# A threshold search inside an attention: the counts, the totals and the update take other places in the queues

## What is computed

```python
def _topk_mask(ck, k):
    probs = jax.nn.softmax(ck, axis=-1)
    _, idx = jax.lax.top_k(probs, k)
    b = jnp.arange(probs.shape[0])[:, None]
    return jnp.zeros_like(probs).at[b, idx].set(1.0)
...
new_mask = _topk_mask(ck, ITER_SIZE)
combined = jnp.clip(history + new_mask, 0.0, 1.0)
novelty = (combined - history).sum(axis=1).mean() / ITER_SIZE
done_next = jnp.logical_or(done, novelty < R)
```

## Time and profile before

| | |
|---|---|
| median of three runs | 1364.15 us (1363.6 to 1365.42) |
| the profiled execution's own time | 1362.49 us |
| its span | 1360.4 us |
| mean granted TensorE clock | 0.967 of full speed |
| TensorE busy | 1226.8 us, 90% |
| VectorE, ScalarE, GpSimd busy | 941.5, 795.5, 577.5 us |

### The profile page before, as it was taken

How to read it: one execution, slowest core, us unless ns; L and a number is a source line. 1 busy time by engine, 2 the same in 40 slices (tenths; PEclk the granted TensorE clock), 3 DMA queues, 4 the chain that set the end, 5 groups by cost and what they waited for, 6 DMA issues and landing times. The chain is left out here.

```text
span 1360.4 us, 37961 instructions
## 1 busy us (share of the span) xinstructions
PE 1226.8 (90%) x13719; PEld 877.9 (65%) x13719; DVE 941.5 (69%) x2042; ACT 795.5 (58%) x2101; POOL 577.5 (42%) x613
## 2 busy tenths in 40 slices
PE   1799999999999986969888888499999979999996
PEld 0466666666666653437766677378888857777775
DVE  6466766767767754758989889489999966334341
ACT  1588788787787761226776676356666633333332
POOL 3587665665665645022222222343333324333443
PEclk9899999999999997969999999789999989999998
DMA  8000000000000000000000000200000000000000
GB/s 213 11 2 1 0 0 0 0 0 0 0 0 0 0 1 1 0 8 10 9 8 8 8 7 7 64 2 1 0 0 0 1 2 9 9 8 8 8 8 17
DMA packets 22740, 14.71 MB, mean 11 GB/s; under 512 B 6378, under 2 KB 21610, under 8 KB 22540
## 3 DMA queue, kind: packets, MB, share of 16 engines
q1 hardware_dynamic: 22520, 13.75, 3.8%
q10 hardware_dynamic: 148, 0.01, 0.0%
HBM read 11.66 MB, written 2.10 MB: 10 GB/s over the span
## 5 line engine op out<-in xcount | busy, mean ns | idle before, releaser
L694 POOL TENSOR_TENSOR r_norm<-ssm,mhalf 128x24 f32<-128x24 f32 x32 | 134.8, 4213 | 161.8 <-DVE ssm L599 161.8
L1929 ACT ACTIVATE moe_hid<-psum 128x512 f32<-128x512 f32 x128 | 76.3, 597 | 136.7 <-PE psum L1863 136.6
L537 ACT ACTIVATE l_probs<-psum,l_n_max 128x248 f32<-128x248 f32 x256 | 117.0, 480 | 57.5 <-DVE l_n_max L617 57.5
L2087 POOL TENSOR_TENSOR moe_acc<-moe_acc,moe_prod 128x512 f32<-128x512 f32 x64 | 81.4, 1272 | 146.4 <-DVE moe_prod L2043 146.4
L1873 PEld LDWEIGHTS psum<-w,moe_hid 128*128 128x128 f32 x1024 | 123.1, 192 | 26.8 <-issue 26.5
L2043 DVE TENSOR_TENSOR moe_prod<-psum,moe_combine 128x512 f32<-128x512 f32 x64 | 44.2, 691 | 134.9 <-PE psum L1873 134.8
L1873 PE MATMUL psum<-w,moe_hid 128*128 128x128 f32 x1024 | 123.4, 275 | 0.0
L1863 PE MATMUL psum<-moe_moe_hT,w 128*128 128x512 f32 x256 | 121.6, 602 | 0.0
L1734 POOL TENSOR_TENSOR l_QX<-l_qT,own_slots 128x512 f32<-128x512 f32 x32 | 33.3, 1040 | 184.0 <-ACT l_qT L1557 184.0
L1734 POOL TENSOR_TENSOR mla_QX<-mla_qT,own_slots 128x512 f32<-128x512 f32 x32 | 33.3, 1040 | 135.5 <-ACT mla_qT L1557 135.5
L701 POOL TENSOR_TENSOR qkn<-qk,r_norm 128x1536 f32<-128x1536 f32 x32 | 88.3, 2761 | 2.5
(11 more groups left out here) (309 smaller groups left out, 3422.3 us busy)
## 6 DMA issues: line engine op xcount, KB each, us to landing
X<-x_in SPq DMA_DIRECT2D x8, 256.0 KB, 4.8
out_dram<-moe_acc SPq DMA_DIRECT2D x32, 64.0 KB, 1.5
CT<-ctx_in SPq DMA_DIRECT2D x8, 240.0 KB, 5.9
l_cT<-ctxT_in SPq DMA_DIRECT2D x32, 60.0 KB, 1.8
w<-w_in SPq DMA_DIRECT2D x1, 1024.0 KB, 5.3
wm<-wm_in SPq DMA_DIRECT2D x1, 768.0 KB, 4.4
wp<-wp_in SPq DMA_DIRECT2D x1, 768.0 KB, 6.5
wkv<-wkv_in SPq DMA_DIRECT2D x1, 512.0 KB, 5.1
```

Source lines behind the costliest of these rows:

```text
L537: e = act.activation(probs[u][:, h, :], psum[:, 2 * u + h // 2, (h % 2) * K:(h % 2 + 1) * K], ACT.Exp, bias=n_max[u][:, h:h + 1], accum_ou ...
L694: pool.tensor_tensor(r_norm[:, :], ssm[:, :], mhalf[:, 0:3 * H], ALU.pow).then_inc(s["norm_inverted"], 1)
L1929: act.activation(hid[i % RING][:, :], psum[:, 2 + i % BANKS, :], ACT.Silu).then_inc(activated[i], 1)
L2087: pool.tensor_tensor(a[:, :, :], a[:, :, :], prod[e % 2][:, :, :], ALU.add).then_inc(summed[e], 1)
```

## The change

The counts get new places on ScalarE: trials 0 and 1 directly behind `exp_b` of the odd step, trial 2 in front of `exp_b` of the even step. On TensorE the total moves from behind `turn_input` to behind the last `multiply_v` of the same even step, in front of `scores`. On VectorE the digit is read between `invert_sums` and `scale_out`; `invert_sums` of an even step now waits for the total as well. The three instructions of `next_trials` leave VectorE; four instructions on GpSimd take their place, each waiting for the one before, at the end of GpSimd's body of the even step. `second_half` stays on VectorE and moves behind `max_a`.

```diff
@@ TensorE @@
-                def total_trials(k, n):
+                def total_trials(k):
                     if round_there(k):
                         wait(pe, tried, k + 1)
-                        wait(pe, out_scaled, n + 1)
                         pe.matmul(psum[:, 6, 3 * P:3 * P + 12], ...
...
                     turn_input(n + 1)
-                    if router and par == 0:
-                        total_trials(k - 1, n - 2)
                     project(n - 2)
...
                     multiply_v(n - 1, 1 - par, 3)
+                    if router and par == 0:
+                        total_trials(k - 1)
                     scores(n + 1, 1 - par)
@@ ScalarE @@
                         if d == 0:
                             wait(act, trials_ready, k)
+                            if isinstance(k, int) and k == ROUNDS:
+                                wait(act, halved, 4)
...
                     copy_k(n + 1, 1 - par)
+                    if router and par == 0:
+                        try_number(k - 1, 2)
                     exp_b(n, par)
                     if router and par == 1:
+                        try_number(k, 0)
                         try_number(k, 1)
                     copy_group(act.copy, act, n, 0)
-                    if router and par == 1:
-                        try_number(k, 2)
                     exp_a(n + 1, 1 - par)
-                    if router and par == 0:
-                        try_number(k, 0)
@@ VectorE @@
-                def read_digit(k, n):
+                def read_digit(k):
                     if round_there(k):
-                        wait(dve, projected, n + 1)
                         wait(dve, totalled, k + 1)
+                        wait(dve, below_made, k)
...
-                def next_trials(k):
-                    if round_there(k):
-                        t = search
-                        wait(dve, trials_ready, k)
-                        wait(dve, digit_read, k + 1)
-                        dve.tensor_scalar(t["bias"][:, :], t["offsets"][:, :], t["below4"][:, :], t["digit4"][:, :], ALU.add, ALU.subtract)
-                        dve.tensor_scalar(t["per_unit"][:, :], t["per_unit"][:, :], 4.0, None, ALU.mult)
-                        i = dve.tensor_scalar(t["below4"][:, :], t["below4"][:, :], t["digit4"][:, :], 4.0, ALU.subtract, ALU.mult)
...
                     copy_group(dve.tensor_copy, dve, n - 1, 3)
-                    if router and par == 0:
-                        read_digit(k - 1, n - 2)
                     add_projection(n - 2)
                     max_b(n, par)
                     take_stats(n - 2)
-                    if router and par == 0:
-                        next_trials(k - 1)
                     shift_b(n, par)
...
+                    if router and par == 0 and round_there(k - 1):
+                        wait(dve, totalled, k)
                     invert_sums(n - 1)
+                    if router and par == 0:
+                        read_digit(k - 1)
                     scale_out(n - 1)
                     max_a(n + 1, 1 - par)
+                    if router and par == 0 and isinstance(k, int) and k == ROUNDS:
+                        second_half()
@@ GpSimd @@
+                def next_trials(k):
+                    if round_there(k):
+                        t = search
+                        wait(pool, digit_read, k + 1)
+                        wait(pool, trials_ready, k)
+                        if isinstance(k, int) and k == ROUNDS:
+                            wait(pool, halved, 4)
+                        pool.tensor_tensor(t["below"][:, :], t["below4"][:, :], t["digit4"][:, :], ALU.subtract).then_inc(below_made, 1)
+                        wait(pool, below_made, k + 1)
+                        pool.tensor_tensor(t["bias"][:, :], t["offsets"][:, :], t["below"][:, :].broadcast_to([P, 3]), ALU.add).then_inc(bias_made, 1)
+                        wait(pool, bias_made, k + 1)
+                        pool.tensor_tensor(t["below4"][:, :], t["below"][:, :], t["four"][:, :], ALU.mult).then_inc(below4_made, 1)
+                        wait(pool, below4_made, k + 1)
+                        pool.tensor_tensor(t["per_unit"][:, :], t["per_unit"][:, :], t["four"][:, :], ALU.mult).then_inc(trials_ready, 1)
...
                     spread_q(n + 1, 1 - par)
+                    if router and par == 0:
+                        next_trials(k - 1)
                     later_scales(n)
```

More of the change, by code:

```diff
@@ L1253, in search_tiles @@
                 tried=sb("tried", [P, 3, Q4], BF16), count=sb("count", [P, 3]), totals=sb("totals", [P, 12]), digit4=sb("digit4", [P, 1]),
-                offsets=sb("offsets", [P, 3]), bias=sb("trial_bias", [P, 3]), below4=sb("below4", [P, 1]), per_unit=sb("per_unit", [P, 1]),
+                offsets=sb("offsets", [P, 3]), bias=sb("trial_bias", [P, 3]), below=sb("below", [P, 1]), below4=sb("below4", [P, 1]), four=sb("four", [P, 1]), per_unit=sb("per_unit", [P, 1]),
                 positive=sb("positive", [P, 1]), sign=sb("sign", [P, 1]), wanted=sb("wanted", [P, 1]), high=sb("high", [P, 1]),
@@ L1350, in _ @@
                     first_trials(dve, t)
+                    dve.memset(t["four"][:, :], 4.0)
                     dve.wait_ge(logits_done, 1)
@@ L1426, in attention16 @@
         halved = sem("halved")
+        below_made = sem("below_made")
+        bias_made = sem("bias_made")
+        below4_made = sem("below4_made")
         def row(T, n):
@@ L1652, in take_stats @@
                         dve.bn_stats(row(stats6, n), row(XO, n)).then_inc(x_stats, 1)
-                def read_digit(k, n):
+                def read_digit(k):
                     if round_there(k):
-                        wait(dve, projected, n + 1)
                         wait(dve, totalled, k + 1)
+                        wait(dve, below_made, k)
                         dve.tensor_scalar(search["totals"][:, :], psum[:, 6, 3 * P:3 * P + 12], search["wanted"][:, :], None, ALU.is_ge,
                                           ALU.add, accum_out=search["digit4"][:, :]).then_inc(digit_read, 1)
-                def next_trials(k):
-                    if round_there(k):
-                        t = search
-                        wait(dve, trials_ready, k)
-                        wait(dve, digit_read, k + 1)
-                        dve.tensor_scalar(t["bias"][:, :], t["offsets"][:, :], t["below4"][:, :], t["digit4"][:, :], ALU.add, ALU.subtract)
-                        dve.tensor_scalar(t["per_unit"][:, :], t["per_unit"][:, :], 4.0, None, ALU.mult)
-                        i = dve.tensor_scalar(t["below4"][:, :], t["below4"][:, :], t["digit4"][:, :], 4.0, ALU.subtract, ALU.mult)
[L1669 to L1673, removed]
                 def second_half():
                     t = search
+                    dve.wait_ge(trials_ready, ROUNDS)
+                    dve.tensor_scalar(t["high"][:, :], t["below4"][:, :], -0.0625, 0.5, ALU.mult, ALU.add).then_inc(halved, 1)
                     dve.wait_ge(halved, 1)
-                    dve.tensor_scalar(t["high"][:, :], t["below4"][:, :], -0.0625, 0.5, ALU.mult, ALU.add).then_inc(halved, 1)
-                    dve.wait_ge(halved, 2)
                     dve.scalar_tensor_tensor(t["low_here"][:, :], t["key"][:, :], t["high"][:, :], t["low"][:, :], ALU.is_equal,
@@ L1682, in second_half @@
                     dve.tensor_scalar(t["above"][:, :], t["key"][:, :], t["high"][:, :], 65536.0, ALU.is_gt, ALU.mult).then_inc(halved, 1)
-                    dve.wait_ge(halved, 4)
+                    dve.wait_ge(halved, 3)
                     dve.tensor_tensor(t["key"][:, :], t["low_here"][:, :], t["above"][:, :], ALU.add)
-                    first_trials(dve, t).then_inc(trials_ready, 1)
+                    first_trials(dve, t).then_inc(halved, 1)
                 def body(n, par, k):
```

## The result

The change takes the median from 1364.8 to 1344.7 us, a ratio of 0.985 (95% interval 0.983 to 0.987).

A forecast was written before the change was run, and what follows sets the result against it. Queues waiting on each other leave TensorE some 32 us idle in the search attention. Savings 5.5 + 1.4 + 2.1 + 2.2 = 11.2 us take 1362.5 to 1351.3; with the median 1.7 above, 1353 us, range 1345 to 1364.

The forecast's parts named there:

- first rival: No new stall: `turn_input` need not wait for GpSimd; double step 13.8 us, gain 31 us, 1333 us; 7%.
- Update on GpSimd: a new stall: Late update delays `centre`, `norm_input`: `turn_input` at t0 + 4.13 (t0: start of the total), not t0 + 2.61; stall 1.52 us.
- fourth rival: Shorter GpSimd waits: gaps 0.08 us instead of 0.16 in the loop, double step 14.9 us, 1348 us; 14%.
- TensorE needs 4.40 us: Time from `turn_input` to `scores` on TensorE, taken as 713.70 - 708.63 - 0.67, used twice in the 15.30 us double step.
- Loop: Eleven double steps in the loops, each 15.30 us instead of 15.80: 11 x 0.50 = 5.5 us less.
- Written out: The two written-out double steps (rounds 0 and 13), 14.87 us instead of 15.56 each: 1.4 us less.
- Second half: The one double step with `second_half`, 15.5 us instead of 17.58: 2.1 us less.
- The end: Rounds 14 and 15, no `turn_input` behind them: waits at the total and most of 0.67 us go, 2.2 us less.
- the forecast of the clock: TensorE's granted clock stays 1.00, stall costs only its length; rival, clock halves behind each stall: up to 62 us, 1415; 2%.
- Update dearer: Rival: GpSimd's four update instructions take 0.40 us each, giving 1364 us (11%), or 0.55, giving 1373 us (8%).
- Count late: Rival: counts late at the total's new place, TensorE waits 0.4 us there in 14 rounds: 5.6 us, 1359 us; 8%.

The follow-up runs named there:

- The late update: The changed kernel with the GpSimd update moved one body later, behind `norm_input` of the odd step, in front of `spread_q`: 1334.2 us, ratio 0.977 to the kernel before.
- the second wait in the experiment: The changed kernel with an already satisfied second wait ahead of the second, third and fourth update instruction: 1346.7 us, 2.0 us more than the change.
- the kernel with the counts alone: The kernel before with only count 0 moved, to stand with count 1 behind `exp_b` of the odd step; total and update as before: 1358.2 us, ratio 0.9955.
- longer update: The changed kernel with four more dependent 128x1 products on GpSimd in the update chain: 1370.7 us, ratio 1.0045 to the kernel before.
- the kernel with the update behind `max_a`: The changed kernel with the update back on VectorE as three instructions, behind `max_a` of the even step, GpSimd's four removed: 1336.6 us, ratio 0.980.

## Why the prediction was right or wrong

**Right: the mechanism.** The three waits go, and one takes their place, of `turn_input` for `norm_input` behind the update. The late update shows that it is the only one in the loop: without it the double step is 13.70 us, where I had 13.8 for my first rival. The stall then costs 14.52 - 13.70 = 0.82 us in a double step, where I had 1.52. The first rival's time, 1333, is what a kernel without the stall really takes (1334.2); it just isn't this change.

**Wrong: the step "Update on GpSimd: a new stall", mis-sized by 0.55 us.** I had `turn_input` at t0 + 4.13; it comes at 702.80 - 699.22 = 3.58. Term by term:

- Reciprocal at t0 + 0.43, not 0.53: 0.10. I took 0.14 us for VectorE to follow TensorE; here it starts 0.04 after the total's modelled end, close behind the copy of the values.
- Digit read by t0 + 1.44, not 1.65: another 0.11. The reading takes 0.14 us from start to end behind a running reciprocal, not the 0.24 of the earlier trace rows, where VectorE had idled in front of it.
- From the first update instruction to `centre` 0.96 us (700.82 to 701.78), not 1.28: 0.32. The instructions took 0.19 to 0.20, as said. The three gaps are 0.08, not the 0.16 of the earlier trace rows: 0.25 of the 0.32. That row has two waits in front of it, the last three of the update one each, and the second wait in the experiment brought most of the difference back. I had named 0.08 as my fourth rival, and gave it 14%. The other 0.07 are the instructions' 0.03 and a `centre` that starts 0.04 before the last of them ends.
- The rest is 0.02.

**Wrong: "TensorE needs 4.40 us", mis-sized by 0.24 in a double step.** I took a step with a wait in it and subtracted the wait. In the change it is shorter: 4.32 from `turn_input` to total (694.90 to 699.22) and 4.24 in the odd step (702.80 to 707.04). The subtraction was not the fault: in the kernel with the counts alone that wait is gone, and the odd step still takes 709.86 - 705.48 = 4.38. The cause of the 0.24 stays open.

**Together** they make 0.55 + 0.24 = 0.79; the double step came 15.30 - 14.52 = 0.78 us below the forecast.

**The sum, by its own terms**, from the input transposes. Loop: 11 x 1.28 = 14.1 us (forecast 5.5). Written out: 222.49 before, 826.07 - 622.22 = 203.85 after, so 18.64 in all; less 14.1 and the second half's 17.58 - (739.12 - 723.93) = 2.39, there remain 2.15 (1.4). Second half 2.4 (2.1). The end, with `project` of the last entry at 863.74 before and 843.80 after: 19.74 - 17.73 = 2.0 (2.2). That is 20.7 against 11.2, and nearly all of the miss is in the loop. Of the 20.7 the spans of the two profiled executions show 1360.4 - 1342.9 = 17.5: the changed kernel comes to this stretch 0.7 us later and takes 2.4 us more behind it, 1.35 of them in the first products of the mixture of experts (6.61 us against 5.26). No run tells why, and the medians' 20.1 is no check on the 20.7.

**The clock: right in the time, weak in the reason.** The granted clock of the changed kernel is 1.00 in the stretch, with its waits of 0.72 us. But I argued from one row, the 2.26 us of the earlier trace rows, that a wait of this kind leaves the clock alone. The longer update's 1.78 us did not, and in the kernel with the counts alone the very same wait, 2.25 us long, dropped it. One execution in which a thing did not happen was no bound, and that the forecast of the clock came true was in part luck. The Trainium skill (TensorE: Matmul & The Clock Gate, section "A second HAM failure mode: psum-queue depth-cycling") warned of a TensorE that stops for moments again and again. The trace of the longer update agrees in part: the clock fell behind 7 of its 14 waits.

**Rivals.** No new stall: wrong, the wait is in the list 14 times. Update dearer: wrong, 0.19 to 0.20 us each. Count late: wrong, no wait at the total. Shorter waits on GpSimd: right for the three gaps inside the update, 0.25 of the 0.55; the gap before the update and the one before `norm_input`, each with two waits, were 0.16. The lower end of my range, 1345, lay 3 us below this rival taken alone; here its gaps, the earlier digit and the shorter steps all went the same way.

## What to carry to other kernels

When work moves to an idle engine, look at what stands behind it in that engine's queue: in front of `centre`, with the digit late, the update cost 10.5 us, and one body later it made no wait in the loop. A chain of small steps is priced by its gaps as much as by its instructions; take the gap from a row with the same number of waits. Waits with different causes nearly add here, so it is worth removing them one by one, and looking each time at what the removal puts in front of something else.

## What was not expected of the hardware

The small VectorE instruction of the update took 0.90 us in the kernel before, but 0.28 at the same shape in the kernel with the update behind `max_a`. The timeline of GpSimd in the kernel before, its last update on VectorE with the listing of all 16 (shortest, median and longest in ns), and VectorE in the other kernel:

```profile
703.80 1.04 POOL L1734 TENSOR_TENSOR l_QX<-l_qT,own_slots 128x512 f32<-128x512 f32 x1 [5.40 <-ACT l_qT L1557]
```

```profile
860.49 0.27 DVE L1666 TENSOR_SCALAR trial_bias<-offsets,below,digit 128x3 f32<-128x3 f32 x1
...
L1666 DVE TENSOR_SCALAR trial_bias<-offsets,below,digit x16: 272/894/901, 625.0 to 860.5; 128x3 f32<-128x3 f32 x16
```

```profile
699.60 0.28 DVE L1672 TENSOR_SCALAR trial_bias<-offsets,below,digit 128x3 f32<-128x3 f32 x1
```

The 0.90 us end at 704.87, and `spread_q` on GpSimd ends at 704.84. In 15 of the 16 rounds of the kernel before the instruction starts while a `spread_q` runs, and takes 0.88 to 0.90; in the last round no `spread_q` is left, and it takes 0.27. So the same kernel shows it with and without, and some 0.6 of the 0.90 us go with GpSimd's instruction. The Trainium skill (SBUF — State Buffer, section "SBUF: two separate sides") says that GpSimd and VectorE share one pair of ports and that the one that starts first holds it for its whole instruction; of VectorE it names instructions in a two-port mode or with two inputs from SBUF. The rows fit that, but whether this instruction is one of those no run shows, so the ports as the cause stay argued.

Behind TensorE's waits the clock fell at some times and not at others: after 1.78 us in rounds 1 to 6 of one execution and not in rounds 8 to 12, after 2.25 us in one kernel and not after 2.26 in another. Where it fell, the step behind it took 1.5 to 2.7 us more.
